# Decay attention: the diagonal block in front of the value product on TensorE, ScalarE and VectorE, and each half tile of maxima in front of its score

## The chip, the cores and the metric

The kernel runs on one core of a Trainium2 chip. The metric is the device time of one launch in microseconds (us). Engines are named as in the profile: PE is TensorE (PEld its weight loads), ACT is ScalarE, DVE is VectorE, POOL is GpSimd, SP is SyncE. PSUM is the accumulator memory that PE writes and that ACT and DVE read; it has eight banks of 512 fp32 columns.

## The reference, cut to what matters

The whole computation is eight residual blocks on 2 x 1024 tokens of width 128. The change touches one of them, the decay attention of the second layer:

```python
q = x @ W_q; k = x @ W_k; v = x @ W_v
latent_kv = (k + v) @ W_down_kv
k_rec = heads(latent_kv @ W_up_k); v_rec = heads(latent_kv @ W_up_v); qh = heads(q)   # 16 heads of 8
scores = jnp.einsum('bhqd,bhkd->bhqk', qh, k_rec) / math.sqrt(d)
decay = jnp.exp(-LAMBDA_DECAY * jnp.abs(t[:, None] - t[None, :]))
scores = scores * decay
attn = jax.nn.softmax(scores, axis=-1)
out = jnp.einsum('bhqk,bhkd->bhqd', attn, v_rec)
out = merge(out) @ W_o
```

The decay factor splits into a rising and a falling exponential, one for keys before the query and one for keys behind it, and each is folded into q and k. Only the 128x128 blocks on the diagonal need both signs, and there the product is corrected by a factor before the exponential.

## The kernel before

The attention runs as two passes that overlap. The heads come in eight groups of four (two batches, four groups each).

Pass one finds each query's largest score, so that the exponential can subtract it. Its work is cut in 256 units. A unit is 128 queries of one head against all 1024 keys: `unit_pe` (matmuls on line 916) writes it as two halves of 512 columns in a pair of banks, in bf16 with 48 rows of the array, and `unit_dve` (line 926) multiplies it by the decay strip and takes the maximum in one DVE instruction. A half whose columns cross the diagonal's edge is written by two matmuls (128+384, 256+256 or 384+128 columns). There are two pairs of banks, so `unit_pe` waits (`p1_free`) until the unit two places back has been read.

Pass two runs in 128 steps, T = 0 to 127, sixteen to a head group. A step is one block of 128 keys against 512 queries for four heads:

- `scores_pe` (L1014) writes one head's score into one of two banks, 50 rows of the array, the two added rows carrying the negated maximum. It waits (`s_free`) until the exponential two scores back is done, since that one read the same bank.
- `exp_act` (L1039) is the exponential on ACT, out to the tile `PT`.
- `pv_pe` (L1030) is the value product of the step before, T - 1, in fp32: four matmuls of 512 columns, or eight of 256, one per head on 32 columns of the array. It waits for all four exponentials of T - 1, and for the diagonal's when T - 1 is even.
- `half_out` (L1050) copies the finished half (eight steps) out of PSUM on ACT. The next half's first `pv_pe` waits for it.

Every even step has a diagonal block. It lives in a bank of its own, 128 columns for each of four heads, and is made in four moves: `diag_pe` (L981, step T - 1) multiplies, `fix_dve` (L1054) applies the correction factor, `diag_max_pe` (L994, step T) subtracts the maxima by a further matmul, and `diag_exp_act` (L1045) takes the exponential. The two PE moves are each four matmuls of 128 columns, in two pairs: heads 0 and 2 sit on array rows 0 to 63, heads 1 and 3 on rows 64 to 127. The second pair waits on the semaphore `dg_even` for the first to have finished, since both write one bank.

At fifteen steps (T = 3, 11, ..., 115, called turns here) the maxima that pass one has collected are turned around: DVE copies them, `maxima_pe` (L935) transposes them into the diagonal's bank, DVE reads them out in two instructions (L949, L951), and SP sends them into the rows that `scores_pe` uses. The next `diag_pe` waits for that read (`m_l`).

Score and unit share PE by halves of the array: the scores of heads 0 and 2 use rows 0 to 63 while the unit beside them uses rows 64 to 127, and the other way round in the second half of a step. PE, ACT and DVE each take their instructions strictly in the order of the program, and the order is written out by hand in `a1_pe`, `a1_act` and `a1_dve`. On ACT a step before the change is four times `exp_act`, then `half_out` where one is due, then `diag_exp_act` in even steps. On DVE it is `fix_dve(T)` in even steps, then two times `unit_dve`, with the two readings of a turn between them. Units last until T = 114; from T = 116 the scores use four banks and the attention's output projection fills the place of the units.

Of the kernel before, what the change touches and what calls it, by code (L numbers as in the profile page):

```python
# [26 lines left out]
GH = 4  # L27
# [77 lines left out]
def build(nc, W, out):  # L105

    ctx = ExitStack()
    with ctx:
# [629 lines left out]
        NSTEP, NUNIT = NGRP * NS, NGRP * NT1  # L738
# [4 lines left out]
        HEADS = (0, 2, 1, 3)  # L743
# [16 lines left out]
        def is_diag(T):  # L760
            return T % 2 == 0
# [244 lines left out]
        def scores_pe(t, T, i):  # L1006
            n, s = divmod(T, NS)
            kt, hf, g, e = key_tile(s), s // NKT, score_head(T, i), GH * T + i
            if T == RING and i >= 2:
                t.wait_ge(p1_free, NUNIT)  # L1010
            elif e >= 2:
                t.wait_ge(s_free, e - (3 if T > RING else 1))
            for v, at, a_, b_ in layout(T)[0]:
                mm = t.matmul(PS[:, score_bank(T, i), at:at + b_ - a_],  # L1014
                              packed(n, g, 2 + v, slice(kt * P, (kt + 1) * P), KP + MROWS),
                              packed(n, g, v, slice(hf * CH + a_, hf * CH + b_), KP + MROWS),
                              start=True, stop=True, skip_group_check=True)
            mm.then_inc(s_s, 1)
# [86 lines left out]
        def a1_pe(t):  # L1105
            a1_prep_pe(t)
            t.wait_ge(a1_v, 1 + NCH)
            for u in range(LEAD):
                unit_pe(t, u, 0)
                unit_pe(t, u, 1)  # L1110
                if u == NTH + 1:
                    maxima_pe(t, 0)
            diag_pe(t, 0, HEADS[0:2])
            diag_pe(t, 0, HEADS[2:4])
            t.wait_ge(a1_neg, 2)
            for T in range(NSTEP):
                n, s = divmod(T, NS)
                u = LEAD + 2 * T
                turn = TURNS.get(T)

                def unit(k, half):
                    if u < NUNIT:
                        unit_pe(t, u + k, half)

                def diag(heads):
                    if is_diag(T):
                        diag_max_pe(t, T, heads)
                    elif T + 1 < NSTEP:
                        diag_pe(t, T + 1, heads)
                if s % NKT == 0:  # L1130
                    t.wait_ge(pk_m, 64 * (T // NKT + 1))
                if s == 0:
                    t.wait_ge(vg_in, n + 1)
                scores_pe(t, T, 0)
                unit(0, 0)
                scores_pe(t, T, 1)
                unit(0, 1)
                if T >= RING:
                    scores_pe(t, T, 2)
                    scores_pe(t, T, 3)  # L1140
                if T == SIXTH_FREE:
                    t.wait_ge(ln_free, 1 + late_count(LN5[0], 1))
                if T == PROJ_FROM:
                    t.wait_ge(p1_free, NUNIT)
                for c, a in PROJ_PE.get(T, ()):
                    project_pe(t, c, a)
                if T > 0:
                    pv_pe(t, T - 1)
                if T < RING:
                    scores_pe(t, T, 2)  # L1150
                unit(1, 0)
                if turn is None:
                    diag(HEADS[0:2])
                else:
                    maxima_pe(t, turn)
                if T < RING:
                    scores_pe(t, T, 3)
                unit(1, 1)
                if turn is not None:
                    diag(HEADS[0:2])  # L1160
                diag(HEADS[2:4])
                if T == LN5_AT:
                    t.wait_ge(x_ready, 1 + NCH * 4 + 2)
                    center_pe(t, LN5[0], 0, 6, XR)
                if T == LN5_AT + 2:
                    variance_pe(t, LN5[0], 0, 6)
                if T == LAST_SUMS:
                    last_sums_pe(t, 2)
            pv_pe(t, NSTEP - 1)
            last_sums_pe(t, 3)  # L1170
            project_pe(t, 3, 0)
            project_pe(t, 3, 1)
            project_pe(t, 3, 2)
            project_pe(t, 3, LAST)

        def a1_act(a):
            a1_prep_act(a)
            for T in range(NSTEP):
                n, s = divmod(T, NS)
                if T >= 2:  # L1180
                    a.wait_ge(pv_free, T - 1)
                for i in range(GH):
                    exp_act(a, T, i)
                if T == LN5_AT:
                    square_act(a, LN5[0], 0, 6)
                if T == LN5_AT + 2:
                    root_act(a, LN5[0], 0, 6)
                if s == NKT:
                    half_out(a, n, 0)
                if s == 0 and n > 0:  # L1190
                    half_out(a, n - 1, 1)
                if is_diag(T):
                    diag_exp_act(a, T)
                if T == LAST_SUMS:
                    last_inverse_act(a, 2)
            half_out(a, NGRP - 1, 1)
            last_inverse_act(a, 3)

        def a1_dve(v):
            a1_prep_dve(v)  # L1200
            for u in range(LEAD):
                unit_dve(v, u)
                if u == NTH - 1:
                    both_sides_dve(v, 0)
                if u == NTH + 1:
                    maxima_dve(v, 0)
            for T in range(NSTEP):
                n, s = divmod(T, NS)
                u = LEAD + 2 * T
                if is_diag(T):  # L1210
                    fix_dve(v, T)
                if T in TURNS:
                    both_sides_dve(v, TURNS[T])
                if u < NUNIT:
                    unit_dve(v, u)
                if T in TURNS:
                    maxima_dve(v, TURNS[T])
                if u < NUNIT:
                    unit_dve(v, u + 1)
                if s == RECIPROCAL_AT and n > 0:  # L1220
                    v.wait_ge(den_in, 16 * n)
                    v.reciprocal(RS, RS).then_inc(den_r, 1)
                for c, a in PROJ_PE.get(T, ()):
                    if a == LAST and c < 2:
                        a1_residual_dve(v, c)
                if T == LN5_AT + 1:
                    centered_dve(v, LN5[0], 0, 6, XN)
                if T == LN5_AT + 4:
                    scale_dve(v, LN5[0], 0, XN)
                if T == LAST_SUMS + 2:  # L1230
                    last_norm_dve(v, 2)
            a1_residual_dve(v, 2)
            last_norm_dve(v, 3)
            a1_residual_dve(v, 3)
# [920 lines left out]
```

## Time and profile before

| | us |
|---|---|
| median of 3 runs | 1193.95 (1192.58 to 1194.89) |
| the profiled execution, own time | 1193.0 |
| its span in the trace | 1191.2 |
| steps T = 0 to 114 (with units), about | 309 to 660 |
| steps T = 115 to 127, about | 660 to 705 |

The profiled execution's own time is 1.8 us more than its span, and 0.95 us under the median. The profile's page lists busy time by engine, the granted clock of PE in tenths of full speed, the chain of work that ended last, and the costliest groups of instructions by line. The busy end of a matmul is modelled, so starts of instructions are the firmer numbers; where the text measures a period it is from start to start.

### The profile page before, as it was taken

How to read it: one execution, taken by the hardware profiler on the slowest of the kernel's cores; microseconds unless marked ns; L12 is line 12 of the kernel's file. 1: busy time of each engine (PE TensorE's matmuls, PEld its weight loads, DVE VectorE, ACT ScalarE, POOL GpSimd, SP SyncE). 2: the span in 40 equal slices, each digit the busy share in tenths (PEclk: the TensorE clock that was granted, in tenths of full speed). 3: DMA queues.
4: the chain of work that ended last, by engine and by line, in shares of the span. 5: the costliest groups of instructions: out<-in, count | busy, mean ns of one | idle time of the engine just before them, and what ended most of it. 6: DMA issues, size and time to landing. Idle time of an engine off the chain costs nothing.

```text
span 1191.2 us, 14247 instructions
## 1 busy us (share of the span) xinstructions
PE 1049.5 (88%) x5224; PEld 399.8 (34%) x5224; DVE 765.8 (64%) x1234; ACT 645.8 (54%) x1098; POOL 185.8 (16%) x107
## 2 busy tenths in 40 slices
PE   5899998986988888888888999998899757999998
PEld 2233333331233332333333333443333222344343
DVE  2677236279999999989998222015599998983200
ACT  4687455262477777777777653326753464413321
POOL 0222800033000000000000000000064213460000
PEclk9899999996799999999999989999899978999999
DMA  7000000069623032130000000000000000000000
GB/s 255 1 1 1 0 0 1 31 236 290 114 37 61 3 60 42 21 61 4 7 8 3 6 1 0 1 0 1 0 1 0 1 0 1 1 0 1 18 1 18
DMA packets 31194, 38.24 MB, mean 32 GB/s; under 512 B 7964, under 2 KB 22300, under 8 KB 30744
## 3 DMA queue, kind: packets, MB, share of 16 engines
q1 hardware_dynamic: 31128, 37.37, 12.5%
q8 instruction: 41, 0.67, 0.2%
q14 instruction: 25, 0.20, 0.1%
HBM read 23.23 MB, written 13.86 MB: 31 GB/s over the span
## 4 chain that ended last, share of the span: by engine, by line
PE 54%; ACT 15%; DVE 10%; issue 3%; DMA 1%; SPq 1%; DVEq 0%; POOL 0%; ACTq 0%
PE PS L1430 17%; PE PS L1030 11%; ACT arena L1039 8%; PE PS L1014 5%; DVE ffn L926 3%; ACT arena L1045 3%; PE PS L1419 2%; PE PS L1420 2%; PE PS L1439 2%; PE PS L916 1%; PE PS L1071 1%; DVE arena L1653 1%; PE PS L1605 1%; PE PS L981 1%; PE PS L1595 1%
## 5 line engine op out<-in xcount | busy, mean ns | idle before, releaser
L926 DVE CUSTOM_DVE_ANT_0 ffn<-PS,XP 128x1024 bf16<-128x1024 f32 x256 | 304.4, 1217 | 29.8 <-PE PS L916 29.8
L1039 ACT ACTIVATE arena<-PS 128x384 f32<-128x384 f32 (+1 forms) x512 | 252.8, 550 | 126.5 <-PE PS L1014 125.4
L916 PE MATMUL PS<-arena 48*128 48x512 bf16 (+3 forms) x704 | 195.4, 344 | 12.4 <-DMA arena<-scr 7.5
L1014 PE MATMUL PS<-arena 50*128 50x512 bf16 (+3 forms) x640 | 157.7, 322 | 18.4 <-ACT arena L1039 11.6
L1030 PE MATMUL PS<-arena 128*32 128x512 f32 (+1 forms) x1280 | 138.3, 521 | 17.8 <-ACT arena L1045 17.6
L1458 ACT ACTIVATE arena<-PS,w_scl 128x512 f32<-128x512 f32 x64 | 43.7, 687 | 157.6 <-PE PS L1430 157.5
L1430 PE MATMUL PS<-arena,w_h1T 128*128 128x512 f32 x256 | 117.8, 606 | 11.3 <-DVE arena L1468 6.6
L1430 PE MATMUL PS<-arena,w_h2T 128*128 128x512 f32 x256 | 114.9, 594 | 0.0
L1014 PEld LDWEIGHTS PS<-arena 50*128 50x128 bf16 x640 | 44.7, 94 | 153.4 <-ACT arena L1039 140.8
L1653 DVE TENSOR_TENSOR_SCAN arena<-arena 128x512 f32<-128x512 f32 x64 | 83.1, 1299 | 0.1
L1682 POOL TENSOR_TENSOR arena<-arena 128x512 f32<-128x512 f32 x32 | 58.6, 1832 | 154.8 <-DVE arena L1661 154.8
L1430 PEld LDWEIGHTS PS<-arena,w_h1T 128*128 128x128 f32 x256 | 48.8, 194 | 73.1 <-issue 56.5
L1475 DVE SCALAR_TENSOR_TENSOR XR<-PS,w_scl,XR 128x512 f32<-128x512 f32 x8 | 6.0, 750 | 101.1 <-PE PS L1439 101.1
L1430 PEld LDWEIGHTS PS<-arena,w_h2T 128*128 128x128 f32 x256 | 48.1, 190 | 59.4 <-issue 55.3
L916 PEld LDWEIGHTS PS<-arena 48*128 48x128 bf16 x704 | 54.3, 97 | 33.5 <-DVE MX L926 21.6
L1054 DVE TENSOR_TENSOR PS<-PS,w_fixT 128x512 f32<-128x512 f32 x64 | 44.3, 692 | 18.9 <-PE PS L981 18.9
L1644 DVE TENSOR_TENSOR arena<-arena,PS 128x512 f32<-128x512 f32 x64 | 42.8, 669 | 18.0 <-PE PS L1589 17.9
L1451 ACT ACTIVATE arena<-PS,w_scl 128x512 f32<-128x512 f32 x32 | 21.8, 687 | 59.5 <-PE PS L1420 59.5
L1030 PEld LDWEIGHTS PS<-arena 128*32 128x32 f32 x1280 | 31.9, 109 | 58.6 <-issue 49.5
L503 DVE TENSOR_TENSOR arena<-arena 128x896 f32<-128x896 f32 (+1 forms) x40 | 43.9, 1138 | 8.4 <-ACT arena L444 7.9
L877 POOL TENSOR_TENSOR arena<-arena 128x1024 f32<-128x1024 f32 x7 | 16.6, 2368 | 206.7 <-DMA arena<-rscr 206.7
L981 PE MATMUL PS<-arena 48*128 48x128 bf16 x256 | 36.2, 222 | 9.4 <-DVE MH L951 8.1
(219 smaller groups left out, 1538.9 us busy)
## 6 DMA issues: line engine op xcount, KB each, us to landing
arena<-scr SPq DMA_DIRECT2D x64, 192.0 KB, 5.8
scr<-arena SPq DMA_DIRECT2D x16, 384.0 KB, 5.3
scr<-arena SPq DMA_DIRECT2D x16, 256.0 KB, 4.7
scr<-arena SPq DMA_DIRECT2D x16, 128.0 KB, 3.1
XP<-xT SPq DMA_DIRECT2D x1, 1024.0 KB, 4.8
w_h1T<-h1T SPq DMA_DIRECT2D x1, 1024.0 KB, 8.1
w_h2T<-h2T SPq DMA_DIRECT2D x1, 1024.0 KB, 8.4
arena<-MH SPq DMA_DIRECT2D x64, 4.0 KB, 1.7
```

Source lines behind the costliest of these rows:

```text
L503: v.tensor_tensor(e, e, window, ALU.mult).then_inc(a0_masked, 1)
L916: mm = t.matmul(PS[:, bank, k0 - lo:k1 - lo], packed(m, g, v, slice(q * P, (q + 1) * P), KP), packed(m, g, 2 + v, slice(k0, k1), KP), star ...
L926: v.tensor_tensor_reduce(JUNK[:, u % 2, :], PS[:, bank:bank + 2, :].rearrange("p a b -> p (a b)"), STRIP[:, at:at + S], 1.0, -3.0e38, ALU. ...
L981: mm = t.matmul(PS[:, D_BANK, g * P:(g + 1) * P], packed(n, g, 2, cols, KP), packed(n, g, 0, cols, KP), start=(g == 0), stop=False, skip_g ...
L1014: mm = t.matmul(PS[:, score_bank(T, i), at:at + b_ - a_], packed(n, g, 2 + v, slice(kt * P, (kt + 1) * P), KP + MROWS), packed(n, g, v, sl ...
L1030: mm = t.matmul(PS[32 * g:32 * g + 32, O_BANK, q:q + b_ - a_], VG[:, n % 2, kt, g, :], PT[:, T % 2, g, a_:b_], start=(s % NKT == 0 and m = ...
L1039: nc.scalar.activation(PT[:, T % 2, score_head(T, i), a0_:a1_], PS[:, score_bank(T, i), a0_:a1_], ACT.Exp).then_inc(s_free, 1)
L1054: v.tensor_tensor(PS[:, D_BANK, :], PS[:, D_BANK, :], fixT[:], ALU.mult).then_inc(dg_fix, 1)
L1430: mm = t.matmul(PS[:, blk, :], (h1T, h2T)[layer][:, kk * HID1 + blk * P:kk * HID1 + (blk + 1) * P], F1_H[F1_IN[layer][j]][:, kk, :], start ...
L1458: nc.scalar.activation(F1_H[F1_OUT[layer][j]][:, blk, :], PS[:, blk, :], ACT.Gelu, scale=scl[:, s0 + blk:s0 + blk + 1]).then_inc(f1_g, 1)
L1653: v.tensor_tensor_scan(h, h, DBX[:, u % 2, :], 0.0 if c % 2 == 0 else HL[:, n:n + 1], ALU.mult, ALU.add).then_inc(m_st, 1)
L1682: nc.gpsimd.tensor_tensor(s[i - 1], s[i - 1], s[i], ALU.add).then_inc(m_pair, 1)
```

## The change

The number of instructions and their sizes stay the same on every engine. Three orders are rewritten.

On PE each half unit stands ahead of its score instead of behind it. The diagonal's matmuls, four in a row, stand behind the second score and ahead of the value product; only in a turn does `diag_pe` stay at the step's end. In a turn, `maxima_pe` goes from behind the third score to directly behind the value product.

On ACT `diag_exp_act` goes from the end of an even step to between its second and third exponential, and with that ahead of `half_out`. On DVE `fix_dve(T + 1)` goes from the start of step T + 1 to between the two units of step T; in a turn it stands behind both units, which is where it stood. `fix_dve(0)` goes ahead of the loop.

```diff
+                unit(0, 0)
                 scores_pe(t, T, 0)
-                unit(0, 0)
+                unit(0, 1)
                 scores_pe(t, T, 1)
-                unit(0, 1)
                 if T >= RING:
                     scores_pe(t, T, 2)
                     scores_pe(t, T, 3)
+                if turn is None:
+                    diag(HEADS[0:2])
+                    diag(HEADS[2:4])
...
                 if T > 0:
                     pv_pe(t, T - 1)
+                if turn is not None:
+                    maxima_pe(t, turn)
+                unit(1, 0)
                 if T < RING:
                     scores_pe(t, T, 2)
-                unit(1, 0)
-                if turn is None:
-                    diag(HEADS[0:2])
-                else:
-                    maxima_pe(t, turn)
+                unit(1, 1)
                 if T < RING:
                     scores_pe(t, T, 3)
-                unit(1, 1)
                 if turn is not None:
                     diag(HEADS[0:2])
-                diag(HEADS[2:4])
+                    diag(HEADS[2:4])
...
-                for i in range(GH):
-                    exp_act(a, T, i)
+                exp_act(a, T, 0)
+                exp_act(a, T, 1)
+                if is_diag(T):
+                    diag_exp_act(a, T)
+                exp_act(a, T, 2)
+                exp_act(a, T, 3)
...
-                if is_diag(T):
-                    diag_exp_act(a, T)
...
+            fix_dve(v, 0)
             for T in range(NSTEP):
                 n, s = divmod(T, NS)
                 u = LEAD + 2 * T
-                if is_diag(T):
-                    fix_dve(v, T)
                 if T in TURNS:
                     both_sides_dve(v, TURNS[T])
                 if u < NUNIT:
                     unit_dve(v, u)
                 if T in TURNS:
                     maxima_dve(v, TURNS[T])
+                elif not is_diag(T) and T + 1 < NSTEP:
+                    fix_dve(v, T + 1)
                 if u < NUNIT:
                     unit_dve(v, u + 1)
+                if T in TURNS:
+                    fix_dve(v, T + 1)
```

PE in step 6, an even step without a turn. L1014 is a score, L916 a half unit, L994 the diagonal's maxima, L1030 the value product of step 5; brackets show the semaphores waited for. Before, from the second score on:

```order
L1014 MATMUL PS<-arena 128x384 [waits s_free]
L916 MATMUL PS<-arena 128x512
L1030 MATMUL PS<-arena 32x512 [waits s_free]
L1030 MATMUL PS<-arena 32x512 x3
L1014 MATMUL PS<-arena 128x384 [waits s_free]
L916 MATMUL PS<-arena 128x512 [waits p1_free]
L994 MATMUL PS<-arena,negb 128x128 [waits dg_fix]
L994 MATMUL PS<-arena,negb 128x128
L1014 MATMUL PS<-arena 128x384 [waits s_free]
L916 MATMUL PS<-arena 128x512
L994 MATMUL PS<-arena,negb 128x128 [waits dg_even]
L994 MATMUL PS<-arena,negb 128x128
```

The same step after, from the half unit ahead of the second score on:

```order
L916 MATMUL PS<-arena 128x512
L1014 MATMUL PS<-arena 128x384 [waits s_free]
L994 MATMUL PS<-arena,negb 128x128 [waits dg_fix]
L994 MATMUL PS<-arena,negb 128x128
L994 MATMUL PS<-arena,negb 128x128 [waits dg_even]
L994 MATMUL PS<-arena,negb 128x128
L1030 MATMUL PS<-arena 32x512 [waits s_free]
L1030 MATMUL PS<-arena 32x512 x3
L916 MATMUL PS<-arena 128x512 [waits p1_free]
L1014 MATMUL PS<-arena 128x384 [waits s_free]
L916 MATMUL PS<-arena 128x512
L1014 MATMUL PS<-arena 128x384 [waits s_free]
```

The four L994 moved from behind the value product, where scores and half units lay between them, to ahead of it, in one row; and each L916 moved ahead of its L1014.

ACT in step 8, where a half is finished. L1039 is an exponential of a score, L1045 the diagonal's, L1050 the copy of the finished half. Before:

```order
L1039 ACTIVATE arena<-PS 128x384 [waits s_s,pv_free]
L1039 ACTIVATE arena<-PS 128x384 [waits s_s] x3
L1050 COPY arena<-PS 128x512 [waits pv_free]
L1045 ACTIVATE arena<-PS 128x4x128 [waits dg_m]
L1039 ACTIVATE arena<-PS 128x512 [waits s_s,pv_free]
```

After:

```order
L1039 ACTIVATE arena<-PS 128x384 [waits s_s,pv_free]
L1039 ACTIVATE arena<-PS 128x384 [waits s_s]
L1045 ACTIVATE arena<-PS 128x4x128 [waits dg_m]
L1039 ACTIVATE arena<-PS 128x384 [waits s_s] x2
L1050 COPY arena<-PS 128x512 [waits pv_free]
```

The diagonal's exponential left the end of the step and stands in its middle; the copy is now the step's last instruction.

PE in step 4, the first behind a turn, whose diagonal waits for the maxima to be read. Before, from the second score on:

```order
L1014 MATMUL PS<-arena 128x128 [waits s_free]
L1014 MATMUL PS<-arena 128x256
L916 MATMUL PS<-arena 128x512
L1030 MATMUL PS<-arena 32x512 [waits s_free]
L1030 MATMUL PS<-arena 32x512 x3
```

After:

```order
L1014 MATMUL PS<-arena 128x128 [waits s_free]
L1014 MATMUL PS<-arena 128x256
L994 MATMUL PS<-arena,negb 128x128 [waits dg_fix]
L994 MATMUL PS<-arena,negb 128x128
L994 MATMUL PS<-arena,negb 128x128 [waits dg_even]
L994 MATMUL PS<-arena,negb 128x128
L1030 MATMUL PS<-arena 32x512 [waits s_free]
L1030 MATMUL PS<-arena 32x512 x3
```

The value product of the turn's step now stands behind a wait for `fix_dve` (`dg_fix`), which it did not before.

## Rows read from the trace of the kernel before

**Rows 1.** The page: busy time by engine, and PE's granted clock in 40 slices
```profile
PE 1049.5 (88%) x5224; PEld 399.8 (34%) x5224; DVE 765.8 (64%) x1234; ACT 645.8 (54%) x1098; POOL 185.8 (16%) x107
...
PEclk9899999996799999999999989999899978999999
```

**Rows 2.** Busy time by engine over steps 0 to 114: PE, PEld, DVE, ACT, POOL, clock, DMA
```profile
309.00:660.00 351.00, 307.38 (x2853) 109.63 (x2850) 315.98 (x572) 259.56 (x540) 16.59 (x12) 0.99 0.17 30
```

**Rows 3.** Who waited for whom, steps 0 to 114: us in all, times, longest
```profile
PEld PS L1014 <- ACT arena L1039: 138.5, 300, 0.8
...
DVE ffn L926 <- PE PS L916: 27.5, 43, 1.8
```

**Rows 4.** The chain over an ordinary pair of steps: start us, us, what
```profile
445.23 1.07 PE PS L1030 x16
...
446.66 1.09 ACT arena L1039 x2
...
448.19 1.00 PE PS L1030 x8
...
449.49 0.87 ACT arena L1039 x2
450.36 0.50 ACT arena L1045
...
450.99 1.06 PE PS L1030 x8
```

**Rows 5.** PE in order of time, same pair: start, us, line, operands
```profile
447.80 0.33 PE L1014 MATMUL PS<-arena 50*128 50x384 bf16 x1
...
448.12 1.07 PE L1030 MATMUL PS<-arena 128*32 128x512 f32 x8
449.12 0.33 PE L1014 MATMUL PS<-arena 50*128 50x384 bf16 x1
...
449.29 0.32 PE L1014 MATMUL PS<-arena 50*128 50x384 bf16 x1
```

**Rows 6.** The chain over a step with a finished half
```profile
453.95 1.00 PE PS L1030 x8
...
457.20 0.59 PE PS L1030
```

**Rows 7.** The chain over a turn and the step behind it
```profile
438.93 1.07 PE PS L1030 x16
...
440.32 0.23 PE PS L935
...
440.64 0.29 DVE MH L949
...
441.25 0.14 issue
441.38 0.28 PE PS L981 x2
...
442.43 0.55 PE PS L1030
```

**Rows 8.** DVE in order of time, in that turn
```profile
441.17 1.20 DVE L926 CUSTOM_DVE_ANT_0 ffn<-PS,XP 128x1024 bf16<-128x1024 f32 x1
...
442.31 0.68 DVE L1054 TENSOR_TENSOR PS<-PS,w_fixT 128x512 f32<-128x512 f32 x1
```

**Rows 9.** The chain in a late step: four diagonal matmuls, then another
```profile
673.41 0.23 PE PS L981 x2
673.64 0.05 issue
...
673.97 1.91 PE PS L1360 x4
```

**Rows 10.** Two stretches elsewhere in which PE has gaps; columns as in 2
```profile
258.00:272.00 14.00, 8.86 (x30) 4.27 (x30) 12.83 (x19) 10.61 (x20) 8.89 (x9) 1.00 0.81 270
1000.00:1020.00 20.00, 14.58 (x36) 4.97 (x36) 16.95 (x27) 11.90 (x16) 5.63 (x4) 0.83 0.00 0
```

## Prediction
> **What bounds the kernel now.** The page first: PE is busy for 88% of the span, DVE for 64%, ACT for 54%, and PE's clock is granted nearly throughout [rows 1]. That average hides the attention. The busy time of steps 0 to 114 shows PE at 307 and DVE at 316 of 351 us, so both look close to full and ACT at 260 does not [rows 2]. The next view, who waited for whom, corrects this: PE's score loads waited 138.5 us in 300 places for the exponential, never over 0.8 us at once, while DVE waited only 27.5 us for half units [rows 3]. PE's busy time counts scores and units that run beside each other, and its value product is waited for. So I read the chain over one ordinary pair of steps [rows 4]. It is a closed loop through PE and ACT and never enters DVE: value product at 445.23, third and fourth exponential from 446.66, value product at 448.19, exponentials from 449.49, the diagonal's exponential from 450.36, value product at 450.99. A pair takes 450.99 - 445.23 = 5.76 us. DVE's work in it is four units of 1.14 (441.17 to 442.31 in [rows 8]) and one correction of about 0.6, some 5.2 us, inside the 5.76. The bound is the loop: last exponential of a step, second score of the next (it needs that exponential's bank), value product, third score, third and fourth exponential.
>
> **The loop before, with its prices.** Let E be the end of a step's fourth exponential. After an odd step E is 446.66 + 1.09 = 447.75 [rows 4]; the second score starts at 447.80, the value product at 448.12, the third score at 449.12 [rows 5], exponentials run from 449.49 for 0.87. (The chain puts that value product at 448.19, because it follows modelled ends; I sum with 448.12.) So the even step takes 0.05 + 0.32 + 1.00 + 0.37 + 0.87 = 2.61. Then the diagonal's exponential stands last on ACT: value product at 450.99, 0.63 after E = 450.36. From a value product to the next E an odd step takes 447.75 - 445.23 = 2.52, so the odd step is 3.15, and the second score is hidden under the diagonal's exponential. Together 5.76.
>
> **The diagonal ahead of the value product.** The order is strict: the second score cannot start before E, the four matmuls stand behind it, the value product behind them. Four diagonal matmuls in a row ahead of another full matmul take 673.97 - 673.41 = 0.56 [rows 9]: two, a wait for the first pair, two. Nothing in the loop hides them; what waits behind them is the value product, and through it every later score. They start when the score has been issued, 0.17 after its start for 384 columns (449.12 to 449.29 in [rows 5]), by scaling an estimated 0.22 for 512. Even step: 0.05 + 0.17 + 0.56 = 0.78 where 0.37 stood, +0.41. Odd step: 0.05 + 0.22 + 0.56 = 0.83 where 0.63 stood, +0.20. Pair: +0.61.
>
> A page's rule would make that cheaper. The four are 4 x 128 columns; at the 0.17 of 384 columns they would be 0.23 in all, not 0.56, if they streamed. The Trainium skill, "TensorE: Matmul & The Clock Gate", section "Wait — 56ns, not 53.3ns?", says that back-to-back matmuls start N columns over the clock plus some 2.5 ns apart, which by that rule is about 0.22 us for the four. The row has a 0.05 pause in it, at the semaphore between the pairs, and the full latency of each pair, so I take 0.56 and keep 0.23 as a rival.
>
> **The diagonal's exponential in mid-step on ACT.** It costs its 0.50 as before, but lies where ACT had nothing to do: from E the first two exponentials take 0.87 (even steps), the diagonal's matmuls are done by 0.78, so it ends by about 1.4, while the third score is not ready before 0.78 + 1.37 = 2.15. Its gain, the hidden 0.63, is already in the +0.20. Once it is gone, the second score and the diagonal's matmuls are what comes last.
>
> **The copy of a finished half.** Before, it stands between the fourth exponential and the diagonal's: value product to value product 457.20 - 453.95 = 3.25 [rows 6], against 450.99 - 448.19 = 2.80 ordinarily, so it costs 0.45. After, it starts at E, beside the second score and the diagonal's matmuls; 0.45 to 0.6 on ACT lies inside the 0.83. Gain 0.45, fourteen times: -6.3. If that cover were gone, the 6.3 would come back.
>
> **The half units ahead.** The one before the second score starts when the score before it has gone out, before E, and leaves the loop, since the score now is first behind E; the 0.05 + 0.17 above has no unit in it already. The one before the third score runs on the other half of the array, so it costs nothing unless it is in two pieces: then the score is held in the queue until the first piece has gone. Three of eight first halves are split, after 128, 256 and 384 columns, 0.06 + 0.11 + 0.17 over eight = 0.04 a step, 0.08 a pair. None or 0.2 a pair would be the ends. VectorE gets its data no earlier where it matters: the loop does not pass it.
>
> **The turns.** Before, a turn's value product starts at 438.93 and the next at 442.43: 3.50, against 448.19 - 445.23 = 2.96, extra 0.54. After, with P the value product's start in the turn: the transpose stands directly behind it, P + 1.07 instead of P + 1.39 (438.93 to 440.32), so DVE's copy starts at P + 1.39 instead of P + 1.71 (440.64), and the diagonal's product, 0.74 later (441.38), at P + 2.13 [rows 7]. DVE then does a unit, from 0.53 behind the copy (441.17) = P + 1.92, and the correction from 1.14 later = P + 3.06, for 0.68 [rows 8]. With 0.14 for the hand-over to PE (the issue at 441.25 in [rows 7]) the maxima start at P + 3.88. This is the new wait. Behind it on PE stands the whole value product, which did not wait for DVE before; it starts at P + 4.44. An ordinary one would start at P + 2.52 + 0.78 = P + 3.30, so +1.14 here; the turn itself has no diagonal ahead of its value product, -0.40. Extra 0.74 instead of 0.54: +0.20, fourteen times, +2.8. Ends: 0 and +1.0 each.
>
> **Steps 115 to 127.** There the same instructions change places, PE is mostly the bound and four score banks take the pressure off. I count nothing, with 3 us either way. The DMAs for the maxima are issued slightly earlier; nothing in the loop waits for them. POOL and SP are untouched.
>
> **The sum.** Steps 0 to 114 are 57.5 pairs: 57.5 x (0.61 + 0.08) = +39.7. Halves -6.3, turns +2.8. In all +36 us. Against the profiled execution's own 1193.0 that is 1229, and the median of the runs stands 0.95 higher: 1230.
>
> **Rivals.**
>
> *Streaming diagonal.* If the four cost 0.23, each step is 0.33 shorter and a pair 5.76 + 0.69 - 0.66 = 5.79. Then +1.7 - 6.3 + 2.8 = -2, 1192, no measurable change or barely faster. Against it stands the pause in [rows 9]; for it, nothing here but the rule.
>
> *DVE was the pace.* The other side. If DVE, 90% busy in [rows 2], set the pace through the unit banks, the units' earlier place would remove its waits for half units, 27.5 us [rows 3], and the time would be 1194 - 27 = 1167. It decides where a pair's DVE work of 5.2 is longer than the loop. The loop is 5.76 now and longer afterwards, and the chain has no DVE in ordinary steps, so I give it little.
>
> *The clock falls.* A slower loop leaves PE idle for more of the time: 307 of 387 us, 79%, instead of 88%. This trace has PE at 63% in one stretch with the clock full, and at 73% in another with 0.83 of it [rows 10], so it can happen. If a tenth of the pairs ran at 1.2 instead of 2.4 GHz, the PE parts of the loop (two scores 0.39, two diagonals 1.12, two value products 2.0, two third scores about 0.6, 4.1 us a pair) would double there: 5.75 x 4.1 = +24, 1254. The Trainium skill names this, in the same page, section "A second HAM failure mode: psum-queue depth-cycling": frequent micro-idles between matmul groups while cycling through PSUM banks make the clock swing. By that rule the loop before should already suffer from it; the granted 0.99 in [rows 2] speaks against it, and the added idle pieces are no longer than the old ones.
>
> **Chances.** Forecast 0.84; streaming diagonal 0.06, half of it faster; DVE as the pace 0.04; clock 0.06. A measurement of this kernel can tell about 0.2%, 2.4 us, from no change. Faster 0.07, same 0.03, slower 0.90. The forecast's own ends: without the split pieces (-4.6), without extra in the turns (-2.8) and 0.08 less a step for hand-overs I may count double (-9), about 1213; with 0.2 a pair for the pieces (+7) and 0.06 more a step, 1244. That is the range; it leaves out the rivals, 0.16, and is as wide as the unknowns make it.
>
> **What would show it.** In the trace after: value products some 6.45 us apart over an ordinary pair; the four L994 or L981 in a row just ahead of each L1030, 0.56 from the first to the value product; ACT idle before the third exponential, longer than before; the copy L1050 gone from the chain; in the step behind a turn L994 waiting for L1054; DVE's idle up by some 35 us; the clock still at 1.0. It would be wrong if the value product started beside the last diagonal matmuls, if L1014 did not wait for the fourth exponential, or if the chain went through L926.

## The result and the profile after

The changed kernel takes 1271.21 us (median of 4 runs, 1268.15 to 1277.12), the kernel before 1194.42 in the runs beside it: 6.5% slower, ratio 1.065, 95% interval 1.061 to 1.069. The direction was forecast with 0.90, but the time lies 41 us above the forecast of 1230 and far outside the range of 1213 to 1244. The loss is 77 us where 36 were summed up.

The page of the kernel after, busy time by engine and the granted clock in 40 slices of 31.7 us, against [rows 1]:

```profile
PE 1127.0 (89%) x5224; PEld 412.9 (33%) x5224; DVE 768.4 (61%) x1234; ACT 656.6 (52%) x1098; POOL 185.8 (15%) x107
...
PEclk8999999985599777799977799999999989999999
```

The instructions are the same and PE is busy 77 us longer, as much as the whole loss. The clock line shows why: slices of 5 and 7 where the kernel before had 9. Steps 0 to 114 now last from 309 to about 740 us. Their busy time, columns as in [rows 2], and the waits in them, as in [rows 3]:

```profile
309.00:740.00 431.00, 388.72 (x2856) 123.86 (x2854) 319.90 (x574) 269.69 (x537) 16.61 (x12) 0.82 0.13 25
```

```profile
DVE ffn L926 <- PE PS L916: 104.5, 71, 2.6
...
PEld PS L994 <- DVE PS L1054: 14.0, 15, 1.1
...
PE PS L994 <- DVE PS L1054: 8.8, 15, 0.6
```

The mean clock fell from 0.99 to 0.82, and there is a wait that was not there before: L994, the diagonal's maxima, for L1054, VectorE's correction, fifteen times, one for each step behind a turn. It is the last two lines, once seen from the weight loads and once from the matmuls. VectorE's busy time hardly changed, and its waits grew from 27.5 to 104.5.

An ordinary pair of steps at full clock, in the chain of the kernel after (start us, us, what), against [rows 4]:

```profile
461.59 0.99 PE PS L1030 x8
...
462.95 1.09 ACT arena L1039 x2
...
464.09 0.33 PE PS L1014
464.43 0.12 PE PS L994 x2
464.55 0.05 issue
464.60 0.28 PE PS L994 x2
464.88 0.99 PE PS L1030 x8
...
468.01 0.55 PE PS L1030
```

From 461.59 to 468.01 are 6.42 us; 6.45 was forecast, 5.76 it was. The score at 464.09 is followed by the four diagonal matmuls, and only then the value product. So the loop was read rightly, and the surprise is elsewhere. The chain over a turn and the steps behind it, against [rows 7]:

```profile
444.92 0.28 DVE MH L951
445.20 1.13 DVE ffn L926
...
446.34 0.62 DVE PS L1054
446.96 0.05 issue
447.01 0.30 PE PS L994 x2
...
447.74 1.86 PE PS L1030 x8
...
452.46 1.86 PE PS L1030 x16
...
457.21 1.86 PE PS L1030 x8
```

Through VectorE's unit and correction the chain comes to the maxima at 447.01, as described. But the value product behind them takes 1.86 us instead of 0.99, and the next ones too. The clock around it, columns as before:

```profile
444.00:447.00 3.00, 1.97 (x23) 0.76 (x17) 2.97 (x8) 1.82 (x5) 0.00 (x0) 1.00 0.03 7
447.00:459.00 12.00, 11.81 (x65) 3.38 (x65) 6.45 (x11) 5.39 (x11) 0.00 (x0) 0.51 0.74 132
459.00:462.00 3.00, 2.94 (x25) 1.07 (x21) 1.93 (x4) 2.03 (x4) 0.00 (x0) 0.69 0.00 0
```

For 3 us TensorE was busy for 1.97 only, at 2.4 GHz. Then it ran for 12 us at 1.2 GHz, although it was busy for 11.81 of them, and came back between 459 and 462. This fall is one of eleven in steps 0 to 114. Each begins within 4 us behind the transpose of a turn; seven last some 14 us, and four last less than 4, such as this one:

```profile
594.00:597.40 3.40, 3.40 (x20) 0.74 (x19) 0.99 (x3) 1.54 (x3) 0.00 (x0) 0.50 0.03 7
```

Together they are some 110 us at half clock. Ahead of them, the first 43 us of the attention, 309 to 352, ran at half clock too, where the kernel before was back at full clock by 315. In the long fall above the value products stand 4.72 and 4.75 us apart (447.74, 452.46, 457.21), against 3.21 on average at full clock: a microsecond at half clock loses (4.73 - 3.21) / 4.73 = 0.32.

### The profile page after: what moved, and what is told of

Its sections match the earlier page's. It is cut to its first block, busy times and chain, and to the rows that moved or that the text cites. A ratio compares the mean times of both kernels' runs of the same rounds, so it can differ in the third digit from the quotient of the medians.

```text
span 1269.0 us, 14248 instructions
## 1 busy us (share of the span) xinstructions
PE 1127.0 (89%) x5224; PEld 412.9 (33%) x5224; DVE 768.4 (61%) x1234; ACT 656.6 (52%) x1098; POOL 185.8 (15%) x107
## 4 chain that ended last, share of the span: by engine, by line
PE 58%; DVE 15%; ACT 8%; issue 3%; DMA 1%; SPq 1%; DVEq 0%; ACTq 0%
PE PS L1436 16%; PE PS L1030 11%; DVE ffn L926 6%; PE PS L1014 6%; PE PS L916 5%; ACT arena L1039 4%; PE PS L994 2%; PE PS L1445 2%; PE PS L981 2%; PE PS L1425 2%; PE PS L1426 2%; DVE arena L1659 1%; PE PS L1071 1%; DVE arena L1650 1%; PE PS L1611 1%
## 5 line engine op out<-in xcount | busy, mean ns | idle before, releaser
L1039 ACT ACTIVATE arena<-PS 128x384 f32<-128x384 f32 (+1 forms) x512 | 254.0, 546 | 189.4 <-PE PS L1014 189.2
L1014 PE MATMUL PS<-arena 50*128 50x512 bf16 (+3 forms) x640 | 175.4, 359 | 22.5 <-ACT arena L1039 19.1
L916 PE MATMUL PS<-arena 48*128 48x512 bf16 (+3 forms) x704 | 183.2, 389 | 12.5 <-DMA arena<-scr 7.6
L1030 PE MATMUL PS<-arena 128*32 128x512 f32 (+1 forms) x1280 | 164.7, 612 | 0.0
L916 PEld LDWEIGHTS PS<-arena 48*128 48x128 bf16 x704 | 53.0, 104 | 146.8 <-issue 69.4
L1014 PEld LDWEIGHTS PS<-arena 50*128 50x128 bf16 x640 | 45.0, 98 | 110.3 <-ACT arena L1039 104.7
L1054 DVE TENSOR_TENSOR PS<-PS,w_fixT 128x512 f32<-128x512 f32 x64 | 44.3, 692 | 26.5 <-PE PS L981 26.5
L994 PE MATMUL PS<-arena,negb 50*128 50x128 bf16 x256 | 39.6, 240 | 13.0 <-DVE PS L1054 9.1
```

The lines of the kernel that those rows point to most:

```text
L916: mm = t.matmul(PS[:, bank, k0 - lo:k1 - lo], packed(m, g, v, slice(q * P, (q + 1) * P), KP), packed(m, g, 2 + v, slice(k0, k1), KP), star ...
L994: mm = t.matmul(PS[:, D_BANK, g * P:(g + 1) * P], negb[row0(g):row0(g) + KP + MROWS, :], packed(n, g, 0, cols, KP + MROWS), start=False, s ...
L1014: mm = t.matmul(PS[:, score_bank(T, i), at:at + b_ - a_], packed(n, g, 2 + v, slice(kt * P, (kt + 1) * P), KP + MROWS), packed(n, g, v, sl ...
L1030: mm = t.matmul(PS[32 * g:32 * g + 32, O_BANK, q:q + b_ - a_], VG[:, n % 2, kt, g, :], PT[:, T % 2, g, a_:b_], start=(s % NKT == 0 and m = ...
L1039: nc.scalar.activation(PT[:, T % 2, score_head(T, i), a0_:a1_], PS[:, score_bank(T, i), a0_:a1_], ACT.Exp).then_inc(s_free, 1)
L1054: v.tensor_tensor(PS[:, D_BANK, :], PS[:, D_BANK, :], fixT[:], ALU.mult).then_inc(dg_fix, 1)
```

## The experiments

Two theories and a rival. T: the new wait behind a turn leaves TensorE idle, and that brings the clock down. U: the half units ahead of their scores do it. R: the slower loop does it everywhere. Each kernel below is the changed one or the one before with the edit shown; the kernels with repeated matmuls do added work and leave none out. Clocks, stretches and counts of falls are those of the one execution of each kernel that was profiled. Ratios are to the kernel before in the same runs.

**One half of the change each.** First the diagonal's part without the units' part:

```diff
-                unit(0, 0)
                 scores_pe(t, T, 0)
-                unit(0, 1)
+                unit(0, 0)
                 scores_pe(t, T, 1)
+                unit(0, 1)
```

(and the same for the second unit).

> Only one half of the change: the diagonal's matmuls ahead of the value product, its exponential in mid-step, its correction between the units, the transpose directly behind the value product; the half units stay behind their scores as before. Theory T (the wait for the correction behind a turn leaves TensorE idle, and its clock falls to half for some 12 us each time): the wait is there, so most of the loss is, 1260 to 1272, with some fourteen stretches at a granted clock of 0.5. Rival U (the half units ahead of their scores spoil the pairing of matmuls and with it the clock): no falls, 1194 + 31 = about 1225. Rival R (the clock falls because the slower loop leaves TensorE too little work everywhere): as T in time, but with falls in ordinary steps too.

Measured: 1257.81, ratio 1.055 (1.052 to 1.059), 2 us under T's range and far above U's 1225. Its trace has eleven falls in steps 0 to 114, all behind turns and none in ordinary steps. Then the units' part alone, in the kernel before:

```diff
+                unit(0, 0)
                 scores_pe(t, T, 0)
-                unit(0, 0)
+                unit(0, 1)
                 scores_pe(t, T, 1)
-                unit(0, 1)
```

> Only the other half: half units ahead of their scores, all else as before. Theory T: no wait was added, the clock stays at 1.0 in steps 0 to 114, 1194 to 1200 (0.04 us a step for units in two pieces, +4.6). Rival U: falls of the clock and over 1220.

Measured: 1190.73, ratio 0.9986 (0.9973 to 0.9999), clock 0.99 over the steps. U falls. The half units ahead of their scores cost nothing that can be told; 4.6 us of loss had been counted, and they came out about 2 us faster. Part of that 2 may be the clock as well, since this execution has 9 us at half clock and the kernel before 14.

**The wait removed.** The changed kernel with the order of before in the step behind each turn only. There the diagonal's pairs stand behind the third and the fourth score again, and its exponential at the end of ScalarE's step:

```diff
-                if turn is None:
+                if turn is None and T - 1 not in TURNS:
                     diag(HEADS[0:2])
                     diag(HEADS[2:4])
```

> The changed kernel, but in the step behind each turn (T = 4, 12, ...) the diagonal's maxima and exponential stand where they stood before, so that TensorE no longer waits for the correction ahead of the value product. Theory T: the falls behind turns go, the loop stays as slow as forecast, 1225 to 1240, the upper part if the slow start (312 to 352 us at half clock) stays. Rival R: falls stay, 1260 or more.

Measured: 1213.17, ratio 1.017 (1.015 to 1.019). That is 58 us faster than the changed kernel by a change in 15 of 128 steps, and faster than the 1225 to 1240 expected. Steps 0 to 114:

```profile
309.00:682.00 373.00, 333.13 (x2852) 113.52 (x2850) 318.70 (x572) 265.87 (x540) 16.61 (x12) 0.98 0.15 28
```

The clock is back at 0.98: there is no fall between 322 us and the end of these steps, and the slow start ends at 321 instead of 352. The removed wait was also worth time of its own: over the step behind a turn and the next one it is 6.58 us from value product to value product here, against 7.54 in the changed kernel where its clock stays full, some 13 us over fourteen turns. The expectation had counted nothing for it. The ordinary steps are the changed kernel's slow ones, value products at 465.29, 468.42 and 471.71, 6.42 a pair:

```profile
465.29 0.99 PE PS L1030 x8
...
468.42 1.00 PE PS L1030 x8
...
471.71 0.99 PE PS L1030 x8
```

So R falls: the slower loop, without the wait, keeps its clock.

**The wait kept, the idleness filled.** Removing the wait removes its time too. The opposite keeps the order and adds work; in the fourteen steps behind a turn with units, `unit_pe(t, u, 1, signal)` is issued three times more, and only the last one signals VectorE:

```diff
                 scores_pe(t, T, 1)
+                if T - 1 in TURNS and T < RING:
+                    for k in range(3):
+                        unit_pe(t, u, 1, k == 2)
```

> The changed kernel in its own order, the wait behind a turn kept, but in those fourteen steps the half unit ahead of the second score is written three more times (same operands, same result, 3 x 512 columns, 0.65 us) behind that score, while TensorE would wait. Work is added and no wait removed. Theory T: TensorE's idle piece is filled, the falls go or become rarer, 1230 to 1245. If the wait costs time by itself and not through idleness and clock: 1271 or some microseconds more.

Measured: 1243.68, ratio 1.042 (1.040 to 1.044): 42 added half units make it 28 us faster. Falls still follow seven of the fourteen turns. Then repeated half units in every pause: one ahead of the second score in each step, but four behind that score in the steps behind a turn, and one more in the turn, ahead of its fourth score:

> The changed kernel in its own order with all its waits, and repeated half units (same operands, same result) in every pause of TensorE: one ahead of the second score in ordinary steps, four behind it in the steps behind a turn, one in the turn. Theory T: the clock stays full nearly throughout, and the time is then the forecast's sum without the clock, 1224 to 1234. If fillers delay the scores: more, with the clock full.

Measured: 1233.27, ratio 1.034 (1.032 to 1.037). Busy time and clock of both, first the fourteen steps filled, then all:

```profile
309.00:720.00 411.00, 373.36 (x2914) 125.74 (x2913) 320.22 (x570) 268.76 (x538) 16.57 (x12) 0.89 0.14 25
```

```profile
309.00:702.00 393.00, 358.23 (x3098) 131.54 (x3095) 322.14 (x572) 268.73 (x538) 16.62 (x12) 0.97 0.14 27
```

Some 170 half units in 243 more matmuls than in the changed kernel, 38 us less time, and four falls left. No wait was taken out of the order and work was only added, so the gain comes from the clock, and the clock column shows it. In the two profiled executions some 30 of the microseconds at half clock that are saved lie in the start.

**The wait alone, in the fast loop.** The kernel before, with the diagonal's maxima ahead of the value product only in the fourteen steps behind a turn (and its exponential between ScalarE's second and third there):

```diff
+                if T - 1 in TURNS and T < RING:
+                    diag(HEADS[0:2])
+                    diag(HEADS[2:4])
                 if T > 0:
                     pv_pe(t, T - 1)
```

> The kernel before, with one thing of the change and only in the fourteen steps behind a turn: there the diagonal's maxima stand ahead of the value product (and its exponential in mid-step), so that TensorE waits for VectorE's correction; the other 101 steps are as before. Theory T: the wait alone makes the clock fall, though the loop is the fast one everywhere else: fourteen waits of about 0.9 us are 13 us, plus some 12 us at half clock each, losing a third of it, 50 us: 1240 to 1265. Rival R (the falls need the slower loop of the change as well): only the waits, 1200 to 1212, clock full.

Measured: 1223.58 (1209.69 to 1224.41), ratio 1.025 (1.023 to 1.027): between the two expectations. Three stretches of it, around one turn:

```profile
448.00:451.00 3.00, 1.75 (x21) 0.88 (x23) 2.96 (x6) 1.66 (x5) 0.00 (x0) 1.00 0.02 3
451.00:455.00 4.00, 3.96 (x29) 1.07 (x25) 1.73 (x5) 2.08 (x5) 0.00 (x0) 0.57 0.01 2
455.00:459.00 4.00, 3.67 (x40) 1.19 (x33) 3.69 (x6) 2.61 (x6) 0.00 (x0) 1.00 0.02 6
```

A gap like the changed kernel's (1.75 of 3 us busy) and a fall, with the clock back within 4 us. So the wait is enough to set off falls in the fast loop: T was right on the cause and wrong on the size. It does not do so each time. This execution falls behind seven of the fourteen turns, each time for less than 4 us; the seven turns between have the same wait and no fall. It is also the fastest of five. The others took 1220.53 to 1224.41 with a clock of 0.939 to 0.941 over the span instead of 0.956. By an estimate from these clocks that is some 40 us more at half clock, which at 0.32 is the 13 us between them. So how long the clock is down differs between executions of one kernel. Falls of 14 us and more are seen only in kernels with the slower loop, but so are short ones, and that the loop lengthens them is not shown. In the two kernels that keep their clock the same place shows less of a gap. These are the kernel before, then the one without the wait behind a turn:

```profile
439.50:442.50 3.00, 2.42 (x33) 0.97 (x28) 2.72 (x7) 1.75 (x4) 0.00 (x0) 1.00 0.00 1
```

```profile
449.00:452.00 3.00, 2.57 (x34) 1.17 (x33) 2.93 (x8) 1.89 (x4) 0.00 (x0) 1.00 0.00 0
```

**The start.** The changed kernel ran the attention's first 43 us at half clock, and the kernel before 6 (not the 3 of the expectation). Here steps 0 to 7 have the order of before, the rest is changed:

> The changed kernel, with steps 0 to 7 in the order of before. The changed kernel ran its first 40 us of the attention at half clock, the one before only some 3 us. Theory T: the start warms up as before, and if that is worth a third of 36 us the time is 1255 to 1262; falls behind later turns stay. If the first steps do not matter: 1268 to 1274.

Measured: 1267.46, ratio 1.061 (1.059 to 1.064), between the two ranges and a miss for T: the clock came up at 317, as expected, but was lost again from 337 to 368, and the time at half clock was as long as in the changed kernel. That fall is not behind a turn. It is in step 8, the first in the new order, and there too the diagonal's maxima waited for VectorE's correction, 0.76 us:

```profile
335.39 0.63 PE L994 MATMUL PS<-arena,negb 50*128 50x128 bf16 x4 [0.76 <-DVE PS L1054]
```

```profile
337.00:367.80 30.80, 30.05 (x165) 8.68 (x164) 17.73 (x31) 15.29 (x31) 0.00 (x0) 0.50 0.01 1
```

So a fall can follow this wait without a turn. The changed kernel's late start, though, is not shown to come from the change. The kernel with the filler behind turns and the one below with VectorE's order alone issue the same matmuls as the changed kernel until after 322 us, and in both the clock was back by then.

**VectorE's order alone.** PE and ACT as in the changed kernel; in a turn VectorE corrects the diagonal ahead of its second unit:

```diff
-                elif not is_diag(T) and T + 1 < NSTEP:
+                if not is_diag(T) and T + 1 < NSTEP:
                     fix_dve(v, T + 1)
                 if u < NUNIT:
                     unit_dve(v, u + 1)
-                if T in TURNS:
-                    fix_dve(v, T + 1)
```

> The changed kernel with TensorE's and ScalarE's order untouched; only VectorE, in a turn, does the correction ahead of the second unit instead of behind it. By the prices of the trace the correction is then done at P + 3.4 instead of P + 3.74 and TensorE's wait behind a turn shrinks from 0.6 us to some 0.2. Theory T (the idle piece of TensorE sets off the fall of the clock): fewer or shorter falls, 1235 to 1260. If the falls come from TensorE's order and not from its wait: within 4 us of 1271.

Measured: 1250.29 (1243.88 to 1261.37), ratio 1.045 (1.042 to 1.049): 21 us faster, inside T's range. The wait of L994 for L1054 shrank from 14.0 and 8.8 us to

```profile
PEld PS L994 <- DVE PS L1054: 10.8, 16, 0.9
PE PS L994 <- DVE PS L1054: 5.7, 16, 0.4
```

On PE that is 0.36 us a turn instead of 0.59, where 0.2 was expected. Falls follow seven of fourteen turns instead of eleven of thirteen. The profiled execution, the slowest of four, gained only 9 us, and by its 137 us at half clock against 156 the gain lies in its earlier start, since its fewer falls are longer (up to 27 us). Why the others gained more no trace shows. PE's order is untouched and the time still moved, so the order on PE alone does not set it.

**A better version.** TensorE pauses ahead of the second score, which waits for an exponential. The diagonal's pairs can stand there instead of behind it. In the kernel before, in all steps below 116 that are no turn and not behind one:

```diff
+                diag(HEADS[0:2])
                 scores_pe(t, T, 0)
                 unit(0, 0)
+                diag(HEADS[2:4])
                 scores_pe(t, T, 1)
                 unit(0, 1)
```

with the changes on ACT and DVE in those steps.

> A version meant to beat both: the diagonal's matmuls in two pairs around the first score, ahead of the second score, where TensorE waits for an exponential anyway; its exponential in mid-step, its correction between the units. In the steps behind a turn, and from step 116 on, all is as before; half units behind their scores. By the loop's prices an ordinary odd step loses the 0.63 of the diagonal's exponential for 0.37, a pair 0.26 faster where it is not a turn pair: 43 x 0.26 = 11 us, and some of the 0.45 at halves: 1178 to 1186. Against it: the two pairs need 0.56 and TensorE's pause there is about 0.5, or the clock falls: 1194 or slower.

Measured: 1191.23, ratio 0.9987 (0.9969 to 1.0004), no difference that can be told, and neither of the two expectations. The twelve executions lie in two groups of six, 1187.74 to 1189.14 with a clock of 0.961 to 0.963 over the span, and 1193.32 to 1195.96 with 0.954 to 0.957. The profiled one, 1188.25, is of the faster group; its clock over the steps is 0.99, no less than before, and it gained 5 us instead of the 11 and more expected. So what is missing is the loop's. The chain over the start of an even step:

```profile
434.98 1.14 DVE ffn L926
...
436.12 0.62 DVE PS L1054
436.75 0.05 issue
436.79 0.28 PE PS L994 x2
...
437.86 0.60 PE PS L1030
```

Now the chain runs through VectorE: unit, correction, maxima, value product. Much of the gain on the one loop was eaten by the other, since the correction moved behind a unit on an engine that has 5.2 us of work in every pair. L994 waited for L1054 43 times in these steps, 18.8 us in all and up to 1.4 at once, and the clock did not fall: a wait of TensorE alone is not enough for a fall. With the half units ahead of their scores as well:

> The previous version (diagonal's pairs around the first score) with the half units ahead of their scores as well. In its trace VectorE had become the pace: value products waited for the correction, the correction for a unit, the unit for its half behind a score. Theory: with the unit's second half ahead of the second score VectorE starts each first unit up to 0.4 us earlier in the pairs where it waited, 1182 to 1188. If VectorE's own work is what is left (5.2 us of a pair), or the gain falls in steps where it does not wait: 1188 to 1192, no difference from the version before it.

Measured: 1190.07, ratio 0.998 (0.9967 to 0.9993): faster than before by some 2 us, inside the second range of 1188 to 1192, and the same as the half units ahead by themselves.

**All kernels beside each other.** The time at half clock is worked out from stretches of 4 us between 308 and 788 us, as twice the part of the clock that is missing in each. The last column takes 0.32 us off for each such microsecond above the 14 of the kernel before. Times are those of the profiled executions.

| kernel | us | at half clock, us | us at the clock of before |
|---|---|---|---|
| before | 1193.0 | 14 | 1193 |
| changed | 1270.8 | 156 | 1225 |
| diagonal's part only | 1258.3 | 126 | 1222 |
| filler behind turns | 1250.3 | 95 | 1224 |
| filler everywhere | 1230.7 | 28 | 1226 |
| warm start | 1269.8 | 162 | 1222 |
| correction first in turns | 1261.4 | 137 | 1222 |
| no wait behind turns | 1213.4 | 20 | 1211 |
| before, with the wait | 1209.7 | 31 | 1204 |
| units' part only | 1191.0 | 9 | |
| pairs around the first score | 1188.3 | 9 | |
| the same with units ahead | 1189.9 | 15 | |

Six kernels with the diagonal change and its wait, one of them only from step 8 on, lie between 1231 and 1271 us and fall on 1222 to 1226 once the clock is taken out. So the 0.32 holds over the whole range, and the change by its order alone costs 29 to 33 us.

## Why the prediction was wrong

- **The loop and what bounds it: right.** It closes through PE and ACT, and an ordinary pair takes 6.42, forecast 6.45, with the four diagonal matmuls between second score and value product [rows 4, 5]. From the end of the exponentials (462.95 + 1.09 = 464.04) to the value product at 464.88 the chain has 0.84 where it had 0.44 (447.75 to 448.19), +0.40 against +0.41 forecast. With the streaming rival's 0.23 for the four it would have been +0.1.
- **The half units: too dear.** Counted at +4.6, measured about -2 alone, with the clock's share of that not known.
- **The copy of a finished half: right.** No PE instruction waits for it in steps 0 to 114, so its 0.45 is hidden.
- **The turns: right in size while the clock is full.** Value product to value product over a turn was put at 4.44; the starts on PE are 4.52 apart:

```profile
443.15 1.07 PE L1030 MATMUL PS<-arena 128*32 128x256 f32 x16
...
447.67 1.93 PE L1030 MATMUL PS<-arena 128*32 128x512 f32 x8
```

- **The sum without the clock: nearly right.** Forecast +36; by the table about +30 to +33, and 1233 was measured where fillers held the clock.
- **The clock: this is the step that failed.** The sum has no term for it. The rival was named and priced, but it got only 0.06 because "the added idle pieces are no longer than the old ones". Piece by piece that is so: TensorE's longest idle pieces in ordinary steps are 0.26 us, and behind a turn they are 0.36 and 0.61, against 0.63 before at a finished half. The length of single pieces was the wrong measure. The prediction itself had described a new wait of TensorE behind each turn, priced it at 0.20 us, and did not ask how busy TensorE is around it: 1.97 of 3 us, against 2.42 before. The changed kernel ran 142 us more at half clock, at 0.32 each some 45 us, more than all the terms of the sum together. Some 35 of the 45 are the eleven falls behind turns, and some 12 the late start, which no run ties to the change (behind step 115 the kernel before has 7 us at half clock and the changed one 3). The rival's 24 us was half of the 45 by two errors against each other: a pair at half clock loses 3.05 us (4.72 + 4.75 against 6.42) and not 4.1, and a third of the time was at half clock (142 of 431 us) and not a tenth of the pairs. The trace of before held a warning too. The stretch at 63% that [rows 10] gives as one with the clock full is followed by 2 us without a matmul, and then by half clock up to the attention and 6 us into it:

```profile
272.00:274.00 2.00, 0.00 (x0) 0.00 (x0) 2.00 (x3) 1.00 (x2) 0.73 (x2) 1.00 1.05 199
274.00:309.00 35.00, 27.12 (x81) 6.78 (x82) 32.70 (x56) 1.60 (x4) 5.65 (x6) 0.50 1.08 274
```

- **VectorE as the pace: refuted for this change.** Its waits grew from 27.5 to 104.5. It became true, in part of the steps, in the version with the pairs around the first score.
- **The rule of the Trainium skill.** "TensorE: Matmul & The Clock Gate", section "A second HAM failure mode: psum-queue depth-cycling", says that frequent micro-idles between matmul groups make the clock swing. This case agrees in part. The clock does swing without any long idle piece: there are eleven falls, and ahead of the one shown TensorE's longest idle piece is 0.61 us. But the short idle pieces of every ordinary step did not do it: in the kernel without the wait behind turns they are 0.26 us long and the clock does not fall between 322 us and step 115. I had let the 0.99 of [rows 2] speak against the rule; it only showed that the kernel before does not meet what the falls need.

What stays open is what exactly sets off a fall, what ends one, and why executions of one kernel differ in both. No run separates idle time of TensorE from the other thing that the kernels with falls share: behind a turn of steps 0 to 114 their value products start 4.15 us or more apart, where the others have 3.78 at most.

## What to carry to other kernels

Where a change adds a wait on TensorE, do not judge it by the wait's own length: some 0.6 us of waiting behind a turn went with falls that cost about 2.5 us more a turn (35 us over fourteen). Ask how busy TensorE is around the wait, and then measure, since no busy share told here for certain whether a fall would come. Moving work into a critical loop to take something else out of it has to be summed for every branch of the loop; here the diagonal's exponential left only one step in two, and its matmuls entered both. Repeating a harmless matmul in a pause is a cheap test of whether a loss is the clock's: if added work makes a kernel faster and the granted clock rises with it, it is.

## What the runs showed of the hardware

All falls in steps 0 to 114 follow a place where the diagonal's matmuls stand ahead of the value product and wait for VectorE, or waited there until half units filled the gap; not every such place has a fall. The table has the fourteen turns of all kernels but the warm start, without those where the clock was down already: TensorE's busy time in the emptiest 3 us that begin within 3 us of the transpose, as it is at most turns; the distance from the turn's value product to the next; and how many turns a fall followed.

| kernel | busy in 3 us | value products apart, us | falls |
|---|---|---|---|
| changed | 1.90 | 4.41 to 4.92 | 11 of 13 |
| diagonal's part only | 1.83 | 4.47 to 5.24 | 11 of 14 |
| before, with the wait | 1.74 | 4.60 to 5.02 | 7 of 14 |
| correction first in turns | 2.15 | 4.15 to 4.44 | 7 of 14 |
| filler behind turns | 2.51 | 4.41 to 4.89 | 7 of 14 |
| filler everywhere | 2.68 | 4.53 to 4.70 | 4 of 14 |
| before | 2.42 | 3.40 to 3.78 | none |
| units' part only | 2.42 | 3.36 to 3.78 | none |
| no wait behind turns | 2.57 | 3.17 to 3.46 | none |
| pairs around the first score | 2.06 | 3.36 to 3.78 | none |
| the same with units ahead | 2.35 | 3.36 to 3.78 | none |

Filling the gap made falls rarer, but the busy share does not foretell them. Of the four stretches below, from the kernel before with the wait, the pairs around the first score, the changed kernel and the filler everywhere, the first three were followed by full clock, and the last, the busiest, by a fall:

```profile
474.10:477.10 3.00, 1.39 (x16) 0.59 (x15) 2.73 (x6) 1.60 (x4) 0.00 (x0) 1.00 0.03 6
```

```profile
443.70:446.70 3.00, 2.06 (x25) 0.71 (x22) 3.00 (x6) 2.23 (x5) 0.00 (x0) 1.00 0.03 6
```

```profile
536.90:539.90 3.00, 1.90 (x20) 0.84 (x19) 2.97 (x8) 1.96 (x4) 0.00 (x0) 1.00 0.02 3
```

```profile
404.40:407.40 3.00, 2.73 (x30) 1.73 (x26) 2.71 (x8) 1.96 (x4) 0.00 (x0) 1.00 0.02 3
```

Once down, the clock stayed down for 12 us while TensorE was busy for 11.81 of them, and over the changed kernel's start, while it was busy for 38.55 of 40:

```profile
309.00:349.00 40.00, 38.55 (x207) 11.42 (x209) 25.29 (x46) 19.85 (x39) 0.00 (x0) 0.50 0.36 65
```

In a loop that passes through other engines half clock does not double the time. It cost 0.32 us per microsecond: a value product took 1.86 us instead of 0.99, while two exponentials of 512 columns took 1.08 at half clock and 1.09 at full.
